# Cross-attention on one core: the order of the maximum units around the score products, and later key steps in the query stage

## The reference

```python
q_hk = (hidden_q @ Wq.T).reshape(Bv, Sv, H, K)
q_big = _apply_rope(jnp.einsum('bshk,hkq->bshq', q_hk, w_kc_q), sin_q, cos_q)
kv_r = _apply_rope(kv_c, sin_k[None], cos_k[None])
q_r = jnp.einsum('bshq,hqr->bhsr', q_big, W_qr)
k_r = jnp.einsum('bld,hdr->bhlr', kv_r, W_kr)
attn = jax.nn.softmax(jnp.einsum('bhsr,bhlr->bhsl', q_r, k_r), axis=-1)
ctx_c = jnp.einsum('bhsl,bld->bhsd', attn, kv_r)
ctx_lat = jnp.einsum('bhsd,hkd->bhsk', ctx_c, w_kc_kv)
return ctx_lat.transpose(0, 2, 1, 3).reshape(Bv, Sv, H * K) @ Wo.T
```

## Time and profile before

| | us |
|---|---|
| median of 3 runs (range) | 2975.4 (2970.22 to 2980.25) |
| the profiled execution, its own time | 2967.93 |
| its span, first to last instruction | 2966.1 |
| PE busy over the span | 2656.2 (90%) |
| DVE busy | 1725.8 (58%) |
| ACT busy | 1108.8 (37%) |
| POOL busy | 1794.7 (61%) |
| TensorE's granted clock, mean | 0.954 of full speed |

### The profile page before, as it was taken

One profiled execution on the slowest core, in us unless ns is written; L12 is line 12 of the kernel. 1 busy time (PEld: TensorE's weight loads), 2 busy tenths in 40 slices (PEclk: granted clock), 3 DMA queues, 4 the chain that ended last, 5 costly groups with the idle time before them and its releaser, 6 DMA issues. The chain is left out here.

```text
span 2966.1 us, 46990 instructions
## 1 busy us (share of the span) xinstructions
PE 2656.2 (90%) x15794; PEld 1573.0 (53%) x15794; DVE 1725.8 (58%) x3045; ACT 1108.8 (37%) x1733; POOL 1794.7 (61%) x695
## 2 busy tenths in 40 slices
PE   7999689999799999999999999999999999999488
PEld 4555366767444545555444545454444544455288
DVE  6888577787455455555555555545555555544276
ACT  3332134444223434434434433434434434344133
POOL 1554458888536566765666666766766566767311
PEclk9999789999879999999999999999999999999699
DMA  3000055656622232223222332223222332220111
GB/s 114 17 22 17 20 164 164 180 164 169 162 52 60 65 73 50 55 55 79 59 55 56 69 68 50 55 56 82 54 55 55 69 68 50 56 62 21 36 38 40
DMA packets 310371, 210.37 MB, mean 71 GB/s; under 512 B 200054, under 2 KB 289354, under 8 KB 310176
## 3 DMA queue, kind: packets, MB, share of 16 engines
q1 hardware_dynamic: 310304, 209.51, 29.4%
HBM read 149.98 MB, written 59.48 MB: 71 GB/s over the span
## 5 line engine op out<-in xcount | busy, mean ns | idle before, releaser
L1596 POOL TENSOR_TENSOR x_acc<-x_acc,x_prob 120x1600 f32<-120x1600 f32 (+1 forms) x320 | 1160.5, 3626 | 330.8 <-ACT x_prob L1614 329.4
L1709 DVE TENSOR_REDUCE x_mx<-x_ring 115x1 f32<-115x480 f32 (+3 forms) x1344 | 823.6, 655 | 563.4 <-PE x_ring L1848 563.1
L1614 ACT ACTIVATE x_prob<-x_scores 120x800 f32<-120x800 f32 (+1 forms) x768 | 619.5, 837 | 723.7 <-PE x_scores L1780 715.5
L1800 PE MATMUL x_context<-x_prob,x_kv 120*64 120x400 f32 (+1 forms) x3072 | 627.9, 531 | 0.0
L1848 PE MATMUL x_ring<-x_kh,x_qm 64*115 64x480 f32 (+3 forms) x1344 | 489.9, 445 | 108.7 <-DVE x_mx L1709 50.3
L1848 PEld LDWEIGHTS x_ring<-x_kh,x_qm 64*115 64x115 f32 (+1 forms) x1344 | 199.2, 176 | 356.8 <-DVE x_mx L1709 312.6
L1596 POOL TENSOR_TENSOR x_acc<-x_prob 121x1600 f32<-121x1600 f32 x32 | 114.3, 3572 | 369.4 <-ACT x_prob L1614 369.4
L1780 PE MATMUL x_scores<-x_qh,x_dh 64*120 64x400 f32 (+1 forms) x1536 | 321.3, 398 | 0.3 <-ACT x_prob L1614 0.3
L1800 PEld LDWEIGHTS x_context<-x_prob,x_kv 120*64 120x64 f32 (+1 forms) x3072 | 191.3, 139 | 244.8 <-issue 181.3
L1780 PE MATMUL x_scores<-x_qh,x_dl 64*120 64x400 f32 (+1 forms) x1536 | 278.8, 344 | 0.0
L1780 PE MATMUL x_scores<-x_ql,x_dh 64*120 64x400 f32 (+1 forms) x1536 | 277.8, 343 | 0.0
(11 more groups left out here) (172 smaller groups left out, 3355.6 us busy)
## 6 DMA issues: line engine op xcount, KB each, us to landing
x_kr<-scratch_kr SPq DMA_DIRECT2D x64, 363.0 KB
x_kd<-scratch_kd SPq DMA_DIRECT2D x64, 332.8 KB
x_rden<-scratch_rden SPq DMA_DIRECT2D x68, 200.0 KB, 3.4
scratch_qh<-q_qsh SPq DMA_DIRECT2D x64, 200.0 KB, 3.8
scratch_ql<-q_qsl SPq DMA_DIRECT2D x64, 200.0 KB, 3.8
x_qm<-scratch_qh SPq DMA_DIRECT2D x64, 200.0 KB, 3.3
x_qh<-scratch_qh SPq DMA_DIRECT2D x64, 200.0 KB, 4.9
x_ql<-scratch_ql SPq DMA_DIRECT2D x64, 200.0 KB, 5.4
```

What stands on the lines that cost most here:

```text
L1596: pool.tensor_tensor(acc[0:rows, parity], first, prob[0:rows, c % PR], ALU.add).then_inc(acc_done.sem, 1)
L1614: act.activation(prob[0:rows, c % PR, u * HALF:(u + 1) * HALF].rearrange("p (j s) -> p j s", j=2), psc[0:rows, u, :, 0:BANK], ACT.Exp).the ...
L1709: dve.tensor_reduce(mx[0:block_rows(r), t * MB + r, i:i + 1], ring[0:block_rows(r), bank, 0:b - a], AX.X, ALU.max).then_inc(rg.read[bank], 1)
L1800: mm = pe.matmul(pav[DC * s:DC * s + DC, j, 0:BANK], kv[0:rows, parity, c], prob[0:rows, c % PR, cols], start=c == 0, stop=c == LC - 1)
```

## The change

In cross-attention (`order`): each of the chunks 1 to 10 becomes pair of `max`, scores 0, scores 1, pair of `max`, context. Chunk 0 becomes kT 2, dT 0, out, dT 1, dT 2, context, pair of `max`, scores 0, scores 1; so the pair too many leaves chunk 1 for chunk 0, and dT 2 as well. Chunk 11 and the places of `den` stay. ACT copies the three steps right behind kT 2 and ahead of save_context and the exponentials. DVE does both `normalise` at the end of chunk 11, behind `turn_maxima`.

In the query stage: POOL's first key product and its sum are cut in two halves each, with the counts of their semaphores raised to fit. `key_steps` moves one head pair later, from p = 2, 4, 6 and the next group's 0 to p = 3, 5, 7 and the next group's 1, still behind `rotate_outer`.

```diff
-        k_terms = sig("k_terms", 3 * GB)
-        k_rotated = sig("k_rotated", GB)
+        k_terms = sig("k_terms", 4 * GB)
+        k_rotated = sig("k_rotated", 2 * GB)
...
             def rope_products(k, i):
-                wait(pool, k_rotated.sem, k_rotated.at(k, i))
+                wait(pool, k_rotated.sem, k_rotated.at(k, 2 * i))
                 half = DC // 2
-                pool.tensor_tensor(kt1[:], kraw[:, i % 2], cosk[:], ALU.mult).then_inc(k_terms.sem, 1)
+                for part in (slice(0, LC // 2), slice(LC // 2, LC)):
+                    pool.tensor_tensor(kt1[:, part], kraw[:, i % 2, part], cosk[:, part], ALU.mult).then_inc(k_terms.sem, 1)
...
             def rope_sum(k, i):
-                pool.tensor_tensor(krot[:, i % 2], kt1[:], kt2[:], ALU.add).then_inc(k_rotated.sem, 1)
+                for part in (slice(0, LC // 2), slice(LC // 2, LC)):
+                    pool.tensor_tensor(krot[:, i % 2, part], kt1[:, part], kt2[:, part], ALU.add).then_inc(k_rotated.sem, 1)
...
                     rotate_outer(k, p)
-                    if p % 2 == 0 and p > 0:
-                        key_steps(k, p // 2 - 1)
+                    if p % 2 == 1 and p >= 3:
+                        key_steps(k, (p - 3) // 2)
+                    if p == 1 and not is_first(k):
+                        key_steps(k - 1, GB - 1)
                     if p == 0 and not is_first(k):
-                        key_steps(k - 1, GB - 1)
                         low_absorbed(k - 1, HP - 2)
...
-        order = []
-        for c in range(LC):
-            if c == 0:
-                order.append([("kT", 2), ("out",), ("context",), ("scores", 0), ("scores", 1), ("dT", 0), ("dT", 1)])
-                continue
-            count = 0 if c == LC - 1 else 3 if c == 1 else 2
-            own = [("scores", 0)]
-            own += next(pairs) if count > 0 else []
-            own += [("scores", 1)]
-            own += [u for _ in range(count - 1) for u in next(pairs)]
-            own += [("dT", 2)] if c == 1 else [("mT",), ("kT", 0), ("kT", 1)] if c == LC - 1 else []
-            own += [("context",)]
-            own += [("den", c - 4)] if c in (4, 5) else []
-            order.append(own)
+        order = [[("kT", 2), ("dT", 0), ("out",), ("dT", 1), ("dT", 2), ("context",), *next(pairs),
+                  ("scores", 0), ("scores", 1)]]
+        for c in range(1, LC):
+            last = c == LC - 1
+            order.append([*([] if last else next(pairs)), ("scores", 0), ("scores", 1),
+                          *([("mT",), ("kT", 0), ("kT", 1)] if last else next(pairs)), ("context",),
+                          *([("den", c - 4)] if c in (4, 5) else [])])
...
                         if made_at(n, ("kT", 2)):
                             copy_keys(n, 2)
+                            for i in range(3):
+                                copy_steps(n, 1 - parity, i)
...
-                        if u[0] == "dT":
-                            copy_steps(n, 1 - parity, u[1])
-                        elif u[0] == "kT" and u[1] < 2:
+                        if u[0] == "kT" and u[1] < 2:
                             copy_keys(n, u[1])
...
-                    if c >= LC - 2:
-                        normalise(n, c - (LC - 2))
+                    if c == LC - 1:
+                        for j in range(2):
+                            normalise(n, j)
```

More of the change, by code:

```diff
@@ L924, in load_k @@
             def load_k(k, j):
-                wait(sp, k_terms.sem, k_terms.at(k, 3 * (j - 1)))
+                wait(sp, k_terms.sem, k_terms.at(k, 4 * (j - 1)))
                 rows = d["ctx"][bass.ds(k * GB + j, 1)].rearrange("b l e -> (b l) e")
@@ L1012, in rope_sum @@
             def rope_sum(k, i):
-                pool.wait_ge(k_terms.sem, k_terms.at(k, 3 * (i + 1)))
+                pool.wait_ge(k_terms.sem, k_terms.at(k, 4 * (i + 1)))
                 wait(pool, k_stored[i % 2].sem, k_stored[i % 2].at(k, 32 * (i // 2)))
                 wait(pool, k_diffed.sem, k_diffed.at(k, i - 1))
-                pool.tensor_tensor(krot[:, i % 2], kt1[:], kt2[:], ALU.add).then_inc(k_rotated.sem, 1)
+                for part in (slice(0, LC // 2), slice(LC // 2, LC)):
+                    pool.tensor_tensor(krot[:, i % 2, part], kt1[:, part], kt2[:, part], ALU.add).then_inc(k_rotated.sem, 1)
             def slot(k, parity, more):
@@ L1134, in key_steps @@
             def key_steps(k, i):
-                dve.wait_ge(k_rotated.sem, k_rotated.at(k, i + 1))
+                dve.wait_ge(k_rotated.sem, k_rotated.at(k, 2 * i + 2))
                 wait(dve, k_stored[(i + 1) % 2].sem, k_stored[(i + 1) % 2].at(k, 32 * ((i + 1) // 2)))
```

## The result

The changed kernel takes 2779.35 us (median of 4 runs, 2778.98 to 2780.14) where the kernel before takes 2974.4 (4 runs, 2970.22 to 2980.25): a ratio of 0.9343, 95% interval 0.9327 to 0.936. It is faster, as forecast, and inside the range, but 64 us slower than the 2715 of the forecast. Its profiled execution took 2779.19 us, with a span of 2777.4 and a granted clock of 0.956.

The account below looks back on a forecast made before the run. The PE was taken to set the pace, losing some 1.1 us a chunk exchanging two banks with DVE. 2967.9 - 205 (slots) - 37 (clock) - 20 (queries) + 2 (border) = 2708, median 7.5 above: 2715; range 2680 to 2800.

Parts of the forecast that it names:

- slow-clock rival: Cross stage: stretches at 1.2 GHz stay, in most slots or all, giving 2752 to 2780 us; chance 0.20.
- Middle chunk: Cross-attention, chunks 2 to 10: 3.69 us instead of 4.23, 0.54 less each, 4.9 us a slot.
- POOL next in line: Middle chunks: POOL's additions start 3.75 apart, 0.06 more than the chunk; four buffers and longer chunks absorb it, no cost.
- Chunk 11 and the two `normalise`: Slot's end: chunk 11 falls from 4.70 to about 3.94, 0.76 won; the second `normalise` delays `out` by 0.7.
- rival in which both lose: The first `normalise` also waits for POOL's whole last addition; `out` starts 2.1 late, 43 us more, 2758; chance 0.08.
- Chunks 0 and 1: Slot's start, from kT 2: 13.8 us together instead of 15.20, 1.4 won a slot.
- Clock, -37: Cross stage: 1.1 to 1.2 us a slot lost to stretches at 1.2 GHz goes, 37 us won.
- Border, +2: Slot ahead of the cross stage (n = -1): dT 0, now in front of `out`, waits for its DMA, 2 us lost.
- Query stage, -20: Key steps one head pair later: seven PE stalls for `rotate_outer`, 15.8 us, and some slow clock go, 20 us won.
- key steps blocked more often: Query stage: all 32 key steps meet a POOL run, 25 more stalls of 2.6, 65 us lost, 2800; chance 0.08.
- Smaller POOL pieces: Query stage: if "issued first" counts from the queue, cutting POOL's instructions smaller would by itself win nothing for key steps.
- likeliest case: Whole kernel: the forecast itself, 2715 us; chance 0.52.

Follow-up runs that it names:

- cross stage alone: Cross-attention of the changed kernel with the query stage of the kernel before: 2730.16 us, ratio 0.9196 to the kernel before.
- query stage alone: Query stage of the changed kernel with the cross-attention of the kernel before: 3021.53 us, ratio 1.0171 to the kernel before.
- the pauses at the old place: Changed cross stage, query stage of before, plus two waits of POOL on its own last instruction in each head pair: 2714.53 us, ratio 0.9138.
- the kernel with pauses: Changed kernel plus two waits of POOL on its own last instruction in each head pair: 2728.26 us, ratio 0.9187 to the kernel before.

## Why the prediction was right, and where it was not

The direction and the large term were right for the reason given. That the time lies in the range as well is partly luck: the query stage was forecast with the wrong sign, and the range held the 64 us only because it made room for rivals that did not come about as described. 2779 even falls into the band of the slow-clock rival (2752 to 2780), whose slow stretches are not there.

- *Middle chunk, 3.69 against 4.23.* Right to 0.01. The walk by starts and by the moments at which DVE lets go of a bank gave also the 0.4 by which the second unit is late. With the pair back in its old place the 4.23 came back, and 158 us.
- *POOL next in line, at no cost.* Right, but only just: five additions in a row take 18.50 us, 3.70 each, without idle time between them, and the PE's chunk takes 3.69. So a chunk made shorter on the PE alone should soon wait for POOL; no run here tried it.
- *Denominators.* Right in kind: the second unit of the pair behind a `den` starts 1716.84 - 1715.40 = 1.44 after it, forecast 1.43.
- *Chunk 11 and the two `normalise`.* The wait of kT 1 is gone, as forecast, and the chunk takes 1743.28 - 1739.32 = 3.96, where 3.94 was forecast. (The 0.76 of the forecast is more than the 0.67 of that wait; the difference was never accounted for.) The hole in `out` is 0.24 instead of 0.7: 14 us better over the slots, since the first `normalise` starts 0.2 behind the cast, earlier against POOL's addition than I had drawn it. The rival in which both lose (2758) didn't come about, though both together take 5.68: 1.82 and 3.94, where one of 0.5 to 0.7 and one of 3 to 4 were to be the sign.
- *Chunks 0 and 1.* 13.68 against 13.8. The first `normalise` in front of the cast, put back by itself, costs 52 us, the turns away from `out` 70: each was priced as a small won term (0.76 and 1.4 a slot), and each is worth more than that, because the new order needs them both. The parts of this order are not a sum of single gains.
- *Clock, -37.* Right, and the rival with 0.20 was wrong. Between 920 and 2500 us, no stretch at 1.2 GHz is left in the changed kernel. The slot of the earlier trace rows without such a stretch took 59.37 and a slot now takes 52.52: 6.85 less, 212 us over the slots where 205 was forecast, which leaves 35 of the 247.6 for the stretches. By the Trainium skill's rule (TensorE: Matmul & The Clock Gate, Part 4: PE-mode transpose) the 16 turns ahead of context should have kept them; the traces don't show that here, with the turns in either place. What brought 12 of them back was the `normalise` in front of the cast. Why the turns' old place, with more waiting in each slot, brought none in the execution that was traced, stays open.
- *Border, +2.* It was +9.1. The only term was dT 0's wait for its DMA, 2 us; it waits 4.4, where the PE waited 0.4 for that DMA before. The term was mis-sized. 5.0 of the 9.1 come with the cross stage alone and 2.7 with the query stage alone (its gap is 35.3), where key steps are made and stored a head pair later; the remaining 1.4 is not explained.
- *Query stage, -20.* This is the step that failed: "One head pair later the sum has long been made, and the step no longer sits between the sum and POOL's products. I take the seven stalls as gone." The first half is true, and 24 of the 32 steps show it at 0.88. But a key step is held by whatever POOL runs, not by the sum, and these seven holds ended only with POOL's run. I never asked where in the head pair POOL has a gap. In the trace of before it was to be read: the power at p = 1, and behind it a run that lasts into p = 3. The forecast also misread the count: the steps of 6.36 were six, in the groups 1 to 6, and the first of the PE's seven waits was 0.76. Now seven steps are long, each about twice the 6.36, and they stand in front of `q_xn`, for whose turn the PE has nothing else to do: 7.4 us and then the lower clock, instead of 2.6. The sign "no key step over 3 us" failed. The 20 itself was a little high: with no key step held at all (the pauses at the old place) the last projection came 14 us earlier.
- *The rival "key steps blocked more often"* had the sign and about the size (+65; the stage lost 50.5), but the wrong mechanism: not 25 more stalls of 2.6, but seven of up to 7.4, 53 us of idle PE in place of 16, and 13 us of clock.
- *Smaller POOL pieces "alone would then win nothing".* They even lose 15 us at the old place. The Trainium skill (SBUF — State Buffer, Who interferes with whom) has it that the one issued first has the shared pair; I had concluded that it must count from the queue. The runs show cases of both kinds: of the twelve POOL instructions that started behind 640.56, none let the waiting DVE in, while the step of 544.42 in the kernel before got in behind the first one, without a gap, and so did steps in the kernel with pauses (the one of 611.56, 1.75 us, between two products). With two waits of 0.2 us in each head pair no step was held for more than 0.9. What decides whether a waiting step is let in, the queue's order or the missing gap, these runs don't separate.

The chances: the likeliest case was given 0.52. Each of its cross terms came, and the time was 2779, because the one term that I had read from its effect (seven stalls go) and not from the engine that makes it was wrong.

## What to carry to other kernels

Price a DVE instruction with two SBUF operands next to a busy POOL not by its own time, but by how long it may be held, at worst until POOL's next gap. Look for that gap, and for what uses that gap up, even an instruction of 1 us. If there is none, a wait of POOL on its own last instruction made one here, for 0.2 us; and keep such a DVE instruction away from the one that the PE waits for next. A pair of units that share two banks belongs ahead of a block of work that needs neither, and a step that is moved "past" a stall must be walked on the engine that holds it, in the new place.

## What the runs showed of the hardware

- A waiting DVE instruction with two SBUF inputs was passed over at border after border in a run of POOL instructions of 1.0 to 1.9 us each: 6.36 us, 10.36, 12.92, up to 13.65, where its own time is 0.88. Other such instructions were let in behind the first POOL instruction of a run (1.61 in the kernel before); what decides is not shown. POOL's additions in the cross stage, each of which waits for the one before, never held a `normalise` for more than one of them (3.97 at most).
- A POOL instruction that waits for the one ahead of it on its own engine starts 0.2 us later; with two such waits in each head pair the long key steps are gone.
- `tensor_scalar` on 100x256 elements, with one SBUF tensor as input, is held by POOL too: 3.46 and 3.17 us for four, against 1.37 with POOL idle.
- After an idle wait of 7.4 us the PE worked at 1.2 GHz from 654.83 into the us from 659 to 660 (granted clock 0.64 in it, 1.00 in the next). Shorter waits are no guide by their length alone: with one of 1.9 us in front of kT 1, 12 slots had such a stretch, with three of 0.6 to 1.2 us spread over the slot, none in the execution traced, and in the kernel before, with 0.67 in front of kT 1, 20 had one.
